# A fused pair of transformer blocks on one core: the product of bv and Wo moved on TensorE's line, deeper rings for x1 and h2, and a new order of steps

## The reference, cut to what matters

```python
# block L0
mask0 = 1.0 - all(x == 0, axis=2)
z  = mha(x, x, Wq1, Wk1, Wv1, mask0, causal=True)      # 16 heads of width 8, keys cut at a data-dependent length
x1 = layernorm(x + z, ln1)
z  = mha(x1, context, Wq2, Wk2, Wv2, mask1, causal=False)
x2 = layernorm(x1 + z, ln2)
z  = ((relu(x2 @ fc1_w.T + fc1_b) * mask0) @ fc2_w.T + fc2_b) * mask0
h2 = layernorm(x2 + z, ln3)
# block L1, 16 heads of width 64
q = h2 @ wq + bq;  k = context @ wk + bk;  v = context @ wv + bv
weights = softmax(q k / 8 + fs + fs)                   # fs: 32 x 16 x 64 x 64, given
out = (weights v) @ wo + bo + h2
out = layernorm(out, ln)
```

## Time and profile before

| | |
|---|---|
| median of 3 runs | 414.31 us |
| profiled execution, and its span | 412.68 us, 410.8 us |
| TensorE busy | 347.7 us, 85% |
| VectorE busy | 309.3 us, 75% |
| ScalarE busy | 235.4 us, 57% |
| GpSimd busy | 236.2 us, 57% |
| start of `C.e`, pair 0 and pair 11 | 77.93 and 308.86 us |

### The profile page before, as it was taken

One profiled execution on the slowest core, in us unless ns is written; L12 is line 12 of the kernel. 1 busy time (PEld: TensorE's weight loads), 2 busy tenths in 40 slices (PEclk: granted clock), 3 DMA queues, 4 the chain that ended last, 5 costly groups with the idle time before them and its releaser, 6 DMA issues.

```text
span 410.8 us, 13138 instructions
## 1 busy us (share of the span) xinstructions
PE 347.7 (85%) x5296; PEld 242.4 (59%) x5296; DVE 309.3 (75%) x897; ACT 235.4 (57%) x561; POOL 236.2 (57%) x372
## 2 busy tenths in 40 slices
...
GB/s 179 332 328 4 2 2 0 4 53 2 54 8 53 10 51 10 53 10 52 10 53 10 53 9 53 10 53 10 53 10 53 10 53 8 53 8 2 9 9 6
DMA packets 13180, 17.87 MB, mean 44 GB/s; under 512 B 1600, under 2 KB 10176, under 8 KB 13120
## 3 DMA queue, kind: packets, MB, share of 16 engines
...
...
## 4 chain that ended last, share of the span: by engine, by line
PE 65%; ACT 15%; DVE 8%; issue 4%; POOL 3%; SPq 3%; DMA 2%; POOLq 0%; DVEq 0%
ACT qT L644 8%; PE C_E L535 8%; PE C_E L453 6%; PE C_E L467 6%; PE C_E L526 5%; PE C_E L488 4%; PE C_E L501 4%; PE A_E L362 4%; PE B_E L362 3%; PE B_E L395 3%; ACT A_S L566 2%; PE C_E L512 2%; PE A_X L381 2%; ACT PTc L661 2%; PE A_E L395 2%
## 5 line engine op out<-in xcount | busy, mean ns | idle before, releaser
L899 POOL TENSOR_TENSOR L_ve<-L_mv,cst 128x1 f32<-128x1 f32 x64 | 12.1, 190 | 80.3 <-DVE L_mv L802 80.2
L891 POOL TENSOR_TENSOR A_kblk<-A_qk,cst 128x1024 f32<-128x1024 f32 x16 | 30.3, 1896 | 37.8 <-DVE A_qk L732 37.8
L559 ACT COPY A_qk<-A_J 128x256 f32<-128x256 f32 x16 | 6.0, 372 | 71.8 <-PE A_X L369 67.0
L932 POOL TENSOR_TENSOR Sc<-Sc,mxc 128x512 f32<-128x512 f32 x32 | 33.3, 1042 | 18.6 <-DVE mxc L849 18.6
L644 ACT ACTIVATE qT<-C_E,bq 128x128 f32<-128x128 f32 x128 | 36.0, 369 | 11.4 <-PE C_E L488 11.4
L910 POOL TENSOR_TENSOR L_xg<-L_xh,vec_sb 128x128 f32<-128x128 f32 x64 | 29.1, 455 | 17.3 <-DVE L_xh L811 15.8
L901 POOL TENSOR_TENSOR L_rstd<-L_ve,cst 128x1 f32<-128x1 f32 x64 | 35.2, 549 | 5.0
L467 PE MATMUL C_E<-wv_sb,cTs 128*64 128x512 f32 x128 | 35.2, 628 | 0.8 <-DVE Sc L840 0.8
L941 POOL TENSOR_TENSOR Pc<-Pc,rdc 128x512 f32<-128x512 f32 x32 | 32.8, 1042 | 5.3 <-DVE rdc L859 5.3
L488 PE MATMUL C_E<-x3T,wq_sb 128*128 128x128 f32 x256 | 35.3, 281 | 0.4 <-ACT x3T L636 0.4
L535 PE MATMUL C_E<-wo_sb,C_zT 128*128 128x128 f32 x256 | 33.3, 286 | 1.6 <-ACT C_zT L631 1.4
...
## 6 DMA issues: line engine op xcount, KB each, us to landing
...
```

The costliest lines, as they stand in the source:

```text
L891: tt(a.kblk[:], a.qk[:, 1].unsqueeze(1).to_broadcast([P, 8, P]), at["rmask"].unsqueeze(2).to_broadcast([P, 8, P]), ALU.mult).then_inc(a.s_ ...
L932: tt(v, v, mxc[:, 8 * g:8 * g + 8].unsqueeze(2).to_broadcast([P, 8, S]), ALU.subtract).then_inc(C.s_sub, 1)
```

## The change

Three things change.

`C.bvo` stands later in TensorE's line, behind the values of the first pair: it waits for both `C.v` evictions of pair 0 (`C.s_vs` of 2). `C.k_0` of pair 0 no longer waits for `obias`; `C.x3t` of pair 0 does.

x1 and h2 get six buffers each (`RING = 6`).

The table `TURN` is replaced by one with a number for each step (in pairs; a step of pair n stands at n plus its number). All queues take their order from it.

```diff
+RING = 6
@@
-        x1 = [sb(f"x1_{k}", [P, D]) for k in range(2)]
-        h2 = sb("h2", [P, D])
+        x1 = [sb(f"x1_{k}", [P, D]) for k in range(RING)]
+        h2 = [sb(f"h2_{k}", [P, D]) for k in range(RING)]
@@ def bvo(n):
                 pe.wait_ge(w_out, 16 * 2)
+                pe.wait_ge(C.s_vs, 2)
@@ def c_k(g):
                     if n == 0:
                         pe.wait_ge(w_keys, 16 * 3)
-                        pe.wait_ge(bvo_ready, 2)
@@ def c_x3t(n):
                 if n:
                     pe.wait_ge(L4.s_y, n)
-                tr(C.E[0][:, 0:P], h2[:], ident).then_inc(C.s_x3t, 1)
+                else:
+                    pe.wait_ge(bvo_ready, 2)
+                tr(C.E[0][:, 0:P], h2[n % RING][:], ident).then_inc(C.s_x3t, 1)
@@
-                     "A.gb": gb(L1, lambda n: x1[n % 2][:], (L2.s_y, 1, 2)),
+                     "A.gb": gb(L1, lambda n: x1[n % RING][:], (L2.s_y, 1, RING)),
-                     "B.3gb": gb(L3, lambda n: h2[:], (C.s_x3r, 1, 1), (C.s_x3t, 1, 1)),
+                     "B.3gb": gb(L3, lambda n: h2[n % RING][:], (C.s_x3r, 1, RING), (C.s_x3t, 1, RING)),
@@
 TURN = """
-B.pv_0+2 C.den_0+1 B.gb+2 C.qs_1+1 C.den_1+1 C.sub_0+1 A.sub_0+5 B.qk+3 B.pv_1+2 A.qk+6 C.ks_0+5 C.bvo+5 C.q_0+1
...
+C.loadf=-11.9714543 C.store=-11.0155051 A.q0=-6.4105495 A.nz=-6.3206542 A.qk=-6.2639583 A.qkv=-6.2340084
...
@@
-WORDS = TURN.split()
+PLACE = {w.split("=")[0]: float(w.split("=")[1]) for w in TURN.split()}
-PLAN = sorted((n + k / len(WORDS) - int(w.split("+")[1]) + LATER[w[0]][n], w[0], w[2:].split("+")[0], n)
-              for k, w in enumerate(WORDS) for n in range(PAIRS))
+PLAN = sorted((n + at + LATER[name[0]][n], name[0], name[2:], n) for name, at in PLACE.items() for n in range(PAIRS))
```

More of the change, by code:

```diff
@@ L924, in x3c @@
                     pool.wait_ge(bvo_ready, 2)
-                tt(x3r[:], h2[:], obias[:], ALU.add).then_inc(C.s_x3r, 1)
+                tt(x3r[:], h2[n % RING][:], obias[:], ALU.add).then_inc(C.s_x3r, 1)
             def c_sub(g):
@@ L965 @@
-B.f2+2 C.pt_0+1 C.pt_1+1 B.f3+2 B.exp_0+3 B.3gb+2 A.kblk+6 A.pt_0+5 C.zts_0+1 C.zts_1+1 B.exp_1+3 B.cm+4 A.zts+5
-A.cnt+6 A.st+5 B.pts_0+3 B.pts_1+3 A.pt_1+5 C.gb+0 B.zn+3 B.y+3 C.zt+1 C.x3ts+2 B.st+3 B.q0+4 B.xts+4 C.xh+1
-A.pv_0+5 A.pv_1+5 B.pt_0+3 B.zts+3 A.xh+5 B.xh+3 C.o_0+1 C.o_1+1 C.rstd+1 C.fadd_0+2 A.rstd+5 B.pt_1+3 C.max_0+2
-B.nz+4 B.tr+4 C.obias+6 C.loadf+5 B.rstd+3 C.qs_0+2 A.z+5 C.fadd_1+2 C.max_1+2 C.store+4 B.cut+4 A.max_0+6
-C.x3t+2 A.q0+7 B.v+4
+C.loadf=-11.9714543 C.store=-11.0155051 A.q0=-6.4105495 A.nz=-6.3206542 A.qk=-6.2639583 A.qkv=-6.2340084
@@ new lines @@
+A.m0=-6.1801246 A.cut=-6.1221183 A.e0=-6.0763234 A.cnt=-5.9504413 A.v=-5.9372431 A.kblk=-5.8906437
+A.max_0=-5.6726237 A.max_1=-5.6485751 A.sub_0=-5.6054737 A.sub_1=-5.5934271 A.exp_0=-5.3722390
+A.exp_1=-5.2997216 A.e=-5.2942035 C.k_0=-5.2084011 A.pt_0=-5.1634077 C.ks_0=-5.1307910 C.k_1=-5.1290296
+A.pts_0=-5.1065163 A.zn=-5.1007177 C.ks_1=-5.0731925 A.pt_1=-5.0608415 A.y=-5.0388478 A.st=-5.0309345
+A.pts_1=-4.9438649 A.xh=-4.8907068 A.pv_0=-4.8670768 A.pv_1=-4.8545353 A.rstd=-4.8523624 A.zts=-4.7461792
```

21 lines of the change are left out of this document (18 added, 3 removed).

## The result

The changed kernel took 421.83 us (median of 4 runs, 420.42 to 423.24), the kernel before 413.99 in runs beside it (4 runs). The ratio is 1.0186, 95% interval [1.0141, 1.0231]: slower by some 1.9%. The profiled execution took 420.42 us with a span of 418.1. The likeliest value, 415.0 with no change clear of noise, did not come. Of the three outcomes slower had been given most (0.40), and the time lies within the range of 406 to 423, 1.2 us from its end. Both profiled executions lie some 1.3 us under the medians (412.68 and 420.42), so their spans compare like the medians.

What follows compares the result with a forecast made beforehand. The prediction took TensorE to bound the even part by a small margin, and chains of waits the ends. Start -3.4, even part +8.9, drain -5.8 gave -0.3; plus 1.0, +0.7 us: median 415.0, range 406 to 423.

Steps and rivals of the forecast that it cites:

- The likeliest case: Whole kernel: the loop binds, 411 to 419 us, likeliest 415.0; chance 0.48.
- the even part: Eleven equal periods, `C.fadd_0` of pair 0 to pair 11: 20.99 us each becomes 21.8, +8.9 us in all.
- the start: Program start to `C.fadd_0` of pair 0: 75.8 us instead of 79.16, -3.4 us; bounds -8 to 0.
- the drain: `C.fadd_0` of pair 11 to the end: shorter by 5.8 us; bounds -2 to -7.
- The loop: Even part: `C.fadd_0`, `C.k_0`, `C.o`, `C.y`, next `C.fadd_0` sets the period, 21.8 us.
- the slow 1.2: Start: TensorE's slow opening matmuls now fall on `A.e` of pair 0, adding 1.2 us.
- the last leg: Start, `A.e` of pair 3 to `C.fadd_0` of pair 0: 23.7 us, 18.0 before.
- The 1.0 that I added: Allowance of 1.0 us in the sum for half a chance of a slow TensorE stretch in the opening.
- The bare chain: Drain without waits for VectorE's moved work: periods of 20.2, 18.6, 18.1 and 17.9 us.
- That the loop does not bind: Rival, even part: period stays at 20.99 us, sum -8.2, 406.1 us; chance 0.22.
- That the clock falls in the even part: Rival: half-clock stretches behind the gap at `C.k_0`, about 2.8 us each; in one period of three, 425; chance 0.16.
- That the opening gains nothing: Rival, start: other waits replace the 11.9 us, +4.1 us, 418.4 us; chance 0.14.

Runs made afterwards that it cites:

- 3: The changed kernel plus one unused 0.6 us VectorE reduction a period, 11 in all, just ahead of `C.fadd_0`: 442.64 us, ratio 1.0639 to the kernel before.
- 4: The changed kernel plus one unused 0.6 us VectorE reduction a period, 11 in all, ahead of `C.y`: 421.29 us, ratio 1.0116 to the kernel before.
- Number 7: The changed kernel plus 18, 20 and 8 unused TensorE transposes in the opening: 415.63 us, ratio 1.0012 to the kernel before.
- Number 12: The program of Number 7 plus unused transposes ahead of TensorE's waits in the drain: 410.06 us, ratio 0.9901 to the kernel before.
- number 1: The kernel before with only x1 and h2 given six buffers each: 415.13 us, ratio 1.0005 to the kernel before.

## Why the prediction was right or wrong

**The likeliest case and its sum.** The mechanism of the even part held, the sum did not: -0.3 was +7.3, and the median went up by 7.8 us, not 0.7. The time is within the range because the range took in the bounds of each term, and all three came out towards the slow one. Two of the three terms, the start and the drain, were missed by some 3 us each and in the same direction, for one reason, TensorE's clock; had the range been a little narrower, it would not have held the result.

**The loop: right.** Forecast 21.8 us a period (21.5 to 22.1), measured 21.90; +9.99 us for +8.9. Its halves were 13.04 and 7.8 + 0.24 and came out as 12.95 and 8.22; TensorE's wait was put at 1.5 to 2 us and is 1.41. Numbers 3 and 4 show that it binds: 0.6 us of work costs 0.6 a period inside the loop (and more where the clock falls for it) and nothing outside. Failed was only the count of VectorE's half, 0.2 short.

**The start: the step on TensorE's speed failed.** `A.e` of pair 0 came at 13.53 (forecast 13.2). "Plus the slow 1.2" took the slow matmuls for one stretch, at the first `A.e`. There were further ones (granted clock 0.50), up to 30 us and from 40.7 to 43, both in or behind stretches in which TensorE mostly waited for a round of A: `A.e` of pair 3 came at 55.02 instead of 52.1. Number 7 has neither stretch, `A.e` of pair 3 at 52.29 and `C.fadd_0` at 76.20, where 75.8 was forecast, so the rounds themselves had been followed rightly; so had the last leg, from `A.e` of pair 3 to `C.fadd_0`, 23.7 forecast and 23.89 measured. -3.4 + 2.7 is -0.7, against -0.25. The 1.0 that I added for half a chance of a slow stretch was this; numbers 3 and 4 have two such stretches as well, and longer ones. That the bound was named as 0 (another slow stretch) saved the range.

**The drain: the chain was right, its speed was not.** The bare chain gave 20.2, 18.6, 18.1 and 17.9. Number 12, in which TensorE is kept at its higher level, has 20.14, 18.77, 17.97 and 17.67, and 17.1 to the end, where I had left the 20.1 of before with the half clock that it contains. Without the transposes, a half-clock stretch followed the gap of 2.44 us ahead of `C.k_0` (1.41, and about 1.0 of `A.qkv`, which has run out by then), and another the gaps of 0.57 to 1.68 us of the last period but one. I had taken away the waits that led to the old stretch and assumed that no new one would open.

**The rivals.** That the loop does not bind is refuted by 3 and 4. That the clock falls in the even part did not happen (1.00 from 78.91 to 319.84), but number 3 shows it come in 0.6 us further on, at 24.1 us a period. Its price had been put at 2.8 us a stretch; measured are 1.3 to 1.6. That the opening gains nothing was put at 0.14 and is close to what happened (-0.25), for one of the reasons named, slow matmuls in each round; of the waits that I had named beside them only that for x shows (1.72 us on VectorE ahead of `A.m0`), and the forecast of `A.e` had it in.

**What the trace of before could not tell** is that its own opening was the better of two forms (number 1). Against the other form, 82.29, the start of the changed kernel's profile is 3.4 us shorter; that this is the forecast figure is luck, since the changed kernel's own opening moves by as much (78.91, and 80.69 and 82.17 in numbers 4 and 3). The span difference of two profiles (7.3) and that of the medians (7.8) agree because both profiles caught executions faster than the median.

The Trainium skill, "TensorE: Matmul & The Clock Gate", Part 1, has the throttled level as the default that activity releases. The rows agree in both ends of the program: with unused matmuls in the gaps (numbers 7 and 12) the mean granted clock rises from 0.957 to 0.969 and to 0.997.
